# One tile's receptance projected from two scaled inputs, a clamp taken into Relu and maximum, and scan columns filled by GpSimd: a layer of RWKV time mixing and a gated feed-forward block on one Trainium2 core

## The reference

```python
x = x + attn(layernorm(x));  x = x + ffn(layernorm(x))

# attn: x_prev is x shifted by one token, zero at the start
xk = x*tmk + x_prev*(1-tmk);  xv = x*tmv + x_prev*(1-tmv);  xr = x*tmr + x_prev*(1-tmr)
k, v, r = xk @ Wk.T, xv @ Wv.T, sigmoid(xr @ Wr.T)
# recurrence over tokens, per channel, p starts at -inf, q at 0
new_p     = max(p, u + k_t)
scale_old = exp(max(p - new_p, -30));  scale_cur = exp(max(u + k_t - new_p, -30))
wkv_t     = (scale_old*q + scale_cur*v_t) / (scale_old + scale_cur + 1e-9)
new_p2    = max(p + w, k_t)
q         = exp(max(p + w - new_p2, -30))*q + exp(max(k_t - new_p2, -30))*v_t
p         = new_p2
out       = (r * wkv) @ Wo.T

# ffn: ternary weights, hidden size 1024
h = silu(x@W1 * s1) * (x@W2 * s2);  h = gelu(h@H1 * sh1);  h = gelu(h@H2 * sh2);  out = h@W3 * s3
```

## Time and profile before

| what | value |
|---|---|
| time, median of 3 runs | 1485.84 us (1485.73 to 1486.19) |
| profiled execution | 1485.31 us |
| its span in the trace | 1483.6 us |
| TensorE busy | 1473.6 us, 99% of the span |
| VectorE busy | 1205.3 us, 81% |
| ScalarE busy | 1077.1 us, 73% |
| GpSimd busy | 204.3 us, 14% |
| memory read and written | 250.76 MB and 33.03 MB |

### The profile page before, as it was taken

How to read it: one execution, slowest core, us unless ns; L and a number is a source line. 1 busy time by engine, 2 the same in 40 slices (tenths; PEclk the granted TensorE clock), 3 DMA queues, 4 the chain that set the end, 5 groups by cost and what they waited for, 6 DMA issues and landing times.

```text
span 1483.6 us, 28137 instructions
## 1 busy us (share of the span) xinstructions
PE 1473.6 (99%) x10326; PEld 1324.7 (89%) x10326; DVE 1205.3 (81%) x1554; ACT 1077.1 (73%) x1626; POOL 204.3 (14%) x173
## 2 busy tenths in 40 slices
PE   8999999999999999999999999999999999999999
PEld 6989898998989989899898989989899898998998
DVE  7797887868888687887878878788886878878655
ACT  6895776867768777686867868677587776868655
POOL 1314020110201102011030210202011020110200
PEclk9999999999999999999999999999999999999999
DMA  9977474755737467374674746657475673746654
GB/s 352 380 264 270 148 231 118 222 160 171 242 97 242 125 204 227 106 248 117 203 210 130 235 130 205 176 168 227 103 240 139 193 234 97 250 117 201 192 178 140
DMA packets 94926, 285.28 MB, mean 192 GB/s; under 512 B 9136, under 2 KB 33328, under 8 KB 92976
## 3 DMA queue, kind: packets, MB, share of 16 engines
q1 hardware_dynamic: 86736, 277.01, 57.5%
q0 software_dynamic: 8160, 7.87, 4.5%
HBM read 250.76 MB, written 33.03 MB: 191 GB/s over the span
## 4 chain that ended last, share of the span: by engine, by line
PE 93%; DVE 3%; ACT 2%; issue 1%; POOL 1%; DMA 0%; DVEq 0%; POOLq 0%; ACTq 0%
PE acc L645 27%; PE acc L647 26%; PE att L554 10%; PE acc L619 7%; PE acc L620 7%; PE acc L671 4%; PE acc L673 4%; PE att L577 3%; PE att L533 2%; PE att L620 1%; PE att L619 1%; DVE stage L1724 1%; DVE op_lo L1595 0%; PE acc L773 0%; PE acc L771 0%
## 5 line engine op out<-in xcount | busy, mean ns | idle before, releaser
L645 PE MATMUL acc<-op_hi,ring 128*128 128x256 f32 x3360 | 810.7, 286 | 0.5 <-issue 0.5
L647 PE MATMUL acc<-op_lo,ring 128*128 128x256 f32 x3360 | 788.8, 279 | 0.0
L645 PEld LDWEIGHTS acc<-op_hi,ring 128*128 128x128 f32 x3360 | 632.2, 188 | 18.6 <-issue 17.6
L647 PEld LDWEIGHTS acc<-op_lo,ring 128*128 128x128 f32 x3360 | 632.0, 188 | 11.1 <-issue 10.0
L1595 DVE TENSOR_TENSOR op_lo<-blocks,op_hi 128x1024 fp32r<-128x1024 f32 (+2 forms) x271 | 338.9, 1265 | 98.3 <-ACT op_hi L1007 90.9
L1007 ACT ACTIVATE op_hi<-blocks 128x1024 fp32r<-128x1024 f32 (+2 forms) x263 | 283.7, 1091 | 82.8 <-DVE blocks L1590 74.9
L619 PE MATMUL acc<-x_hi,w_rnd 128*128 128x512 f32 x420 | 167.6, 399 | 0.0
L620 PE MATMUL acc<-x_lo,w_rnd 128*128 128x512 f32 x420 | 165.9, 395 | 0.0
L2018 POOL TENSOR_TENSOR v_sb<-mix_v,v_sb 128x1024 f32<-128x1024 f32 (+1 forms) x19 | 39.4, 2072 | 833.7 <-DVE r_sb L1522 824.8
L1047 ACT ACTIVATE blocks<-acc,vec 128x256 f32<-128x256 f32 x268 | 104.9, 475 | 60.9 <-PE acc L647 60.8
L1047 ACT ACTIVATE blocks<-parts,vec 128x256 f32<-128x256 f32 x240 | 102.3, 497 | 56.2 <-DVE parts L1652 47.9
(11 more groups left out here) (185 smaller groups left out, 2116.8 us busy)
## 6 DMA issues: line engine op xcount, KB each, us to landing
ring<-scratch SPq DMA_DIRECT2D x427, 512.0 KB, 4.2
scratch<-stage SPq DMA_DIRECT2D x11, 1024.0 KB, 12.4
stage<-in_w_ffn SPq DMA_DIRECT2D x10, 1024.0 KB, 10.9
x_in<-in_x SPq DMA_DIRECT2D x32, 256.0 KB, 4.8
out<-x_next SPq DMA_DIRECT2D x30, 256.0 KB, 5.1
out<-mix_v POOLq DMA_DIRECT2D x30, 256.0 KB, 4.4
scratch<-in_w_ffn SPq DMA_DIRECT2D x4, 1024.0 KB, 15.0
ring<-stage SPq DMA_DIRECT2D x7, 512.0 KB, 9.4
```

The costliest lines, as they stand in the source:

```text
L645: pe.matmul(out, act(w), act(op_hi[:, k, c, :]), start=(begins and c == 0 and m % 2 == 0), stop=False, skip_group_check=True)
L647: mm = pe.matmul(out, act(w), act(op_lo[:, k, c, :]), start=False, stop=(c == QC - 1), skip_group_check=True)
```

## The change

Only tile 0 is touched.

- Receptance of the first sequence. Instead of a `mix_r` made by VectorE, ScalarE makes two scaled copies of the transposed x straight from PSUM (`share_r`): x times tmr into `mix_r`, and x shifted by one column times (1 - tmr) into `share`, which lies in `x1_next`. TensorE projects both and adds them up in PSUM, eight matmuls where there were four. VectorE makes 1 - tmr (`rest_r`), and GpSimd sets the first column of `share` to zero. The late sequence's `ln1` moves ahead of the first key copies on ScalarE. A `sem_inc` on VectorE takes the place of the two missing counts of `dve_mix`.
- The clamp of the state's new share, in both sequences. It was a clamp to 0 and 30 on VectorE ahead of Exp(-x). Now ScalarE takes Relu of the exponent, then Exp(-x), and the bound of 30 comes as a maximum with exp(-30) in the multiplication by v. The other clamp on the same exponent comes after both exponents, and waits for Relu.
- The column 0 of `seq` is filled by GpSimd, in both sequences, once with the lowest number and once with zero, where VectorE copied `carry_p` and `carry_q`.

```diff
@@ -34,6 +34,7 @@
 WKV_EPS = 1e-9
 WARM = (17, 1, 9)
 CLAMP = 30.0
+LEAST_GAIN = float(np.exp(np.float32(-CLAMP)))
 LOWEST = float(np.finfo(np.float32).min)
 
 
@@ -207,6 +208,7 @@
         moments = sb("moments", [P, NB, 2])
         var_eps = sb("var_eps", [P, NB])
         minus_half = sb("minus_half", [P, NB])
+        rest_r = sb("rest_r", [P, DC])
         mean_neg = sb("mean_neg", [P, NB])
         rstd = sb("rstd", [P, NB])
         offset = sb("offset", [P, NB])
@@ -278,6 +280,7 @@
             return ap.rearrange("p (b d) -> p b d", b=NB)
 
         now, before = seq[:, :, :, 1:], seq[:, :, :, 0:SEG]
+        share = x1_next[:, 0:DC, 0:SEG]
 
         def ffn_weights(w):
             a = 0
@@ -352,6 +355,8 @@
         st_x1 = tally("st_x1", n_seq, 16)
         dve_last, st_last, pe_block = (ctx.enter_context(nc.semaphore(n)) for n in ("dve_last", "st_last", "pe_block"))
         first_scan = ctx.enter_context(nc.semaphore("first_scan"))
+        first_rest, first_share, first_relu = (ctx.enter_context(nc.semaphore(n)) for n in ("first_rest", "first_share", "first_relu"))
+        first_col = ctx.enter_context(nc.semaphore("first_col"))
         first_wo = ctx.enter_context(nc.semaphore("first_wo"))
         first_x1 = ctx.enter_context(nc.semaphore("first_x1"))
         first_num = ctx.enter_context(nc.semaphore("first_num"))
@@ -545,14 +550,23 @@
                 for j in chunks:
                     which, e = divmod(j, DC)
                     src = (mix_k, mix_v, mix_r)[which]
-                    pe.wait_ge(s.dve_mix.sem, s.dve_mix.at(t, (which + 1) * DC))
+                    if s is FIRST[0] and which == 2:
+                        pe.wait_ge(first_share, 1 + 2 * DC)
+                    else:
+                        pe.wait_ge(s.dve_mix.sem, s.dve_mix.at(t, (which + 1) * DC))
+                    if s is FIRST[0] and which == 1:
+                        pe.wait_ge(first_share, 1 + 2 * DC)
                     if s is WHOLE and j >= 2:
                         pe.wait_ge(s.act_kvr.sem, s.act_kvr.at(t, j - 1))
                     elif j >= 4:
                         pe.wait_ge(s.act_kvr.sem, s.act_kvr.at(t, j - 3))
                     for c in range(DC):
                         mm = pe.matmul(s.banks[KVR_BANK[j]][:, s.cols], wm[:, which, c, e * P:(e + 1) * P], src[:, c, s.cols],
-                                       start=(c == 0), stop=(c == DC - 1))
+                                       start=(c == 0), stop=(c == DC - 1 and not (s is FIRST[0] and which == 2)))
+                    if s is FIRST[0] and which == 2:
+                        for c in range(DC):
+                            mm = pe.matmul(s.banks[KVR_BANK[j]][:, s.cols], wm[:, which, c, e * P:(e + 1) * P], share[:, c, :],
+                                           start=False, stop=(c == DC - 1))
                     s.pe_kvr.add(mm)
 
             def project_out(s, t):
@@ -946,6 +960,14 @@
                 act.wait_ge(s.act_x.sem, s.act_x.at(t, 3))
                 s.act_x.add(act.activation(carry_x[:, :, s.seqs], seq[:, :, s.seqs, SEG:SEG + 1], ACT.Copy))
 
+            def share_r(s):
+
+                act.wait_ge(first_rest, 1)
+                for c in range(DC):
+                    x = s.banks[c][:, s.cols]
+                    act.activation(mix_r[:, c, s.cols], x, ACT.Identity, scale=tmr[:, c:c + 1]).then_inc(first_share, 1)
+                    act.activation(share[:, c, 1:SEG], x[:, 0:SEG - 1], ACT.Identity, scale=rest_r[:, c:c + 1]).then_inc(first_share, 1)
+
             def copy_kvr(s, t, chunks=range(3 * DC)):
                 for j in chunks:
                     which, e = divmod(j, DC)
@@ -958,6 +980,9 @@
 
                 act.wait_ge(s.dve_pre.sem, s.dve_pre.at(t, (1, 2, 3, 4)[k] if isinstance(t, int) and t < 2 else (3, 4, 1, 2)[k]))
                 ap, sign = ((fresh, -1.0), (norm_ch, 1.0), (mix_v, 1.0), (mix_k, -1.0))[k]
+                if s is not WHOLE and k == 0:
+                    act.activation(fresh[:, :, s.cols], norm_ch[:, :, s.cols], ACT.Relu).then_inc(first_relu, 1)
+                    act.wait_ge(first_relu, 1 + FIRST.index(s))
                 s.act_exp.add(act.activation(ap[:, :, s.cols], ap[:, :, s.cols], ACT.Exp, scale=sign))
 
             def exp_r(s, t):
@@ -1164,8 +1189,9 @@
             act.activation(warm_act[:], zeros[:], ACT.Exp)
             ln1(early_seq, 0)
             copy_x(early_seq, 0)
+            share_r(early_seq)
+            ln1(late_seq, 0)
             copy_kvr(early_seq, 0, [0, 1])
-            ln1(late_seq, 0)
             exp(early_seq, 0, 0)
             exp(early_seq, 0, 1)
             copy_kvr(early_seq, 0, range(2, 3 * DC))
@@ -1427,10 +1453,11 @@
 
             def first_running_max(s):
 
+                if s is FIRST[0]:
+                    dve.wait_ge(s.dve_mix.sem, s.dve_mix.at(0, 2 * DC))
+                    dve.sem_inc(s.dve_mix.sem, DC)
                 dve.wait_ge(s.dve_mix.sem, s.dve_mix.at(0))
                 dve.wait_ge(s.act_x.sem, s.act_x.at(0))
-                link(s, dve.tensor_copy(seq[:, :, s.seqs, 0:1], carry_p[:, :, s.seqs]))
-                settle(s, 0)
                 n = s.pairs[0]
                 for c in range(DC):
                     dve.wait_ge(s.pe_kvr.sem, s.pe_kvr.at(0, c + 1))
@@ -1452,8 +1479,11 @@
                 k4, p4 = by_seq(k_sb[:])[:, :, s.seqs], before[:, :, s.seqs]
                 for c in range(DC):
                     if s is not WHOLE:
+                        if c == 0:
+                            dve.wait_ge(first_col, 1 + 2 * FIRST.index(s))
                         dve.wait_ge(s.act_kvr.sem, s.act_kvr.at(t, c + 1))
-                    link(s, dve.scalar_tensor_tensor(by_seq(norm_ch)[:, c, s.seqs], p4[:, c], decay[:, c:c + 1], k4[:, c], ALU.add, ALU.subtract))
+                    done = link if s is WHOLE or c < DC - 1 else lambda s, instruction: s.dve_pre.add(instruction)
+                    done(s, dve.scalar_tensor_tensor(by_seq(norm_ch)[:, c, s.seqs], p4[:, c], decay[:, c:c + 1], k4[:, c], ALU.add, ALU.subtract))
 
             def exponents(s, t):
                 now_exponents(s, t)
@@ -1482,10 +1512,12 @@
             def first_exponents(s, t):
 
                 next_exponents(s, t)
-                settle(s, t)
-                next_clamps(s, t, 0)
                 now_exponents(s, t)
                 settle(s, t)
+                g = norm_ch[:, :, s.cols]
+                dve.wait_ge(s.dve_pre.sem, s.dve_pre.at(t, 1))
+                dve.wait_ge(first_relu, 1 + FIRST.index(s))
+                s.dve_pre.add(dve.tensor_scalar(g, g, 0.0, -CLAMP, ALU.min, ALU.max))
                 now_clamps(s, t, 2)
 
             def gain(s, t):
@@ -1494,13 +1526,19 @@
                 if s is FIRST[0]:
                     dve.wait_ge(s.act_kvr.sem, s.act_kvr.at(t, 2 * DC))
                 new = fresh[:, :, s.cols]
+                if s is not WHOLE:
+                    link(s, dve.scalar_tensor_tensor(new, new, LEAST_GAIN, v_sb[:, :, s.cols], ALU.max, ALU.mult))
+                    return
                 link(s, dve.tensor_tensor(new, new, v_sb[:, :, s.cols], ALU.mult))
 
             def recurrence(s, t, c):
 
                 if c == 0:
                     settle(s, t)
-                    link(s, dve.tensor_copy(seq[:, :, s.seqs, 0:1], carry_q[:, :, s.seqs]))
+                    if s is WHOLE:
+                        link(s, dve.tensor_copy(seq[:, :, s.seqs, 0:1], carry_q[:, :, s.seqs]))
+                    else:
+                        dve.wait_ge(first_col, 2 + 2 * FIRST.index(s))
                 for n in s.pairs:
                     link(s, dve.tensor_tensor_scan(
                         now[:, c, n, :], by_seq(norm_ch)[:, c, n, :], by_seq(fresh[:])[:, c, n, :],
@@ -1771,9 +1809,10 @@
             first_variance(late_seq)
             dve.wait_ge(ld_vec, 16)
             dve.wait_ge(setup_pool, 2)
+            dve.tensor_scalar(rest_r[:], tmr, -1.0, 1.0, ALU.mult, ALU.add).then_inc(first_rest, 1)
             mix_difference(early_seq, 0)
-            for which in range(3):
-                mix(early_seq, 0, which)
+            mix(early_seq, 0, 0)
+            mix(early_seq, 0, 1)
             first_running_max(early_seq)
             first_exponents(early_seq, 0)
             gain(early_seq, 0)
@@ -2057,11 +2096,18 @@
             pool.memset(zeros[:], 0.0)
             pool.memset(carry_x[:], 0.0)
             pool.memset(carry_q[:], 0.0)
+            pool.memset(share[:, :, 0:1], 0.0).then_inc(first_share, 1)
             pool.memset(carry_p[:], LOWEST).then_inc(setup_pool, 1)
             pool.wait_ge(setup_pool, 2)
             for k, s in enumerate(FIRST):
                 first_deviation(s, 1 + k)
             for k, s in enumerate(FIRST):
+                column = seq[:, :, s.seqs, 0:1]
+                pool.wait_ge(s.dve_mix.sem, s.dve_mix.at(0))
+                pool.memset(column, LOWEST).then_inc(first_col, 1)
+                pool.wait_ge(s.dve_pre.sem, s.dve_pre.at(0, 3))
```

(2 more changed lines are left out.)

## The result

The changed kernel takes 1488.3 us (median of 20 runs, 1486.24 to 1490.41), the kernel before beside it 1485.8 us (20 runs, 1484.71 to 1488.52). The ratio is 1.0014, with a 95% interval of 1.0008 to 1.0021. By the medians it is 2.5 us more and by the means 2.1, which lies within the 0.2% (3.0 us) that the prediction took as the bound of "no change". The forecast, 1486.5 us, had the direction right. Its range ended at 1487.6 and does not hold the time.

What follows compares the result with a forecast made beforehand. TensorE, busy 99% of the span, was taken as the bound. Tile 0's delay of +0.66 us grows to +0.87, less 0.2 at the transposes: +0.7, so a median of 1486.5 us, range 1485.2 to 1487.6.

Steps and rivals of the forecast that it cites:

- The first sequence: Tile 0's front: VectorE gains 0.4 to 0.5 us, but the doubled receptance projection makes x1 0.66 us late.
- a loss of this part alone: Relu on ScalarE replacing VectorE's clamp in tile 0: 0.63 us against the clamp's 0.43.
- The second sequence: Tile 0 behind the x1 copy: 0.66 us late grows to +0.87, less 0.2 at the transposes, giving +0.7 us.
- the forecast of +0.87: Second sequence: Exp of the remaining clamp starts 0.87 us late, and the second check frees TensorE as late.
- it will not move: Weight transfer landing at 56.78 us, before the second sequence's transposes: its queue waits for no arithmetic, so it stays put.
- the second wait for a check: TensorE after the transposes: a wait for a load its own matmuls release, so the delay would fill none of it.
- the 0.3 us for op_lo: TensorE's later wait for op_lo, 0.3 us: follows its own earlier work, so the delay would not fill it.
- the prediction's own signs of being wrong: x1 copied before 27.1, TensorE past the transposes before 60.1, or a granted clock below 1.00.
- (1): Tile 0's front keeps its time, gain and loss cancel: 1485.8 us, 1485.4 at best; chance 0.22.
- (2): SyncE's load of tile 1's x, issued at 48.08, moves with transfers behind it: 1487.3 us; chance 0.13.
- (3): TensorE's clock halves at the wait before 51.13 until the transposes, adding 5.9 us: 1492.4 us; chance 0.02.
- (4): Relu brings table loads of 1.28 us each; the instruction order shows none added; chance nil.

Runs made afterwards that it cites:

- e16: The kernel before with feed-forward loads held until the last ring piece lands, plus the change's Relu and GpSimd columns, without the doubled receptance: 1486.19 us.
- e7: The kernel before with half of the second set's receptance projection moved ahead of TensorE's third flag check: 1487.72 us, against 1486.30 for the kernel before.
- the held pair: The kernel before and the changed kernel, both with SyncE's feed-forward loads held until the last ring piece has landed: means 1485.98 and 1486.90 us.
- e3: The kernel before with ten warming matmuls instead of nine ahead of the first output projection: 1486.93 us, ratio 1.0010.
- e2: The kernel before with only the first sequence's receptance from two scaled copies and eight matmuls: 1487.43 us, ratio 1.0011.
- e19: The changed kernel again, unaltered, against the kernel before: 1488.17 us, ratio 1.0005.
- e1: The changed kernel with the first sequence's receptance made as before, Relu and GpSimd's columns kept: 1486.76 us, ratio 1.0005.
- e6: The changed kernel with SyncE holding the feed-forward loads back until the last ring piece has landed: 1486.42 us.

## Why the prediction was right and wrong

**The first sequence, right.** Forecast and measured: exponents of the scan ready for the clamps at 14.55, and Relu started at 14.48; Relu 0.63 for 128x512, exactly as taken from Exp; scaled copies 0.46 to 0.48 each at a pitch of 0.36, against 0.4 taken; second receptance copy done at 18.33 forecast and 18.26 measured; warming from 18.4, measured 18.32; x1 at 27.7, measured 27.64. ScalarE's idle time held the four copies, as said. The scan started at 11.94 after 0.53 us of waiting for the key chunk, also as said. The sentence from the Trainium skill ("ScalarE: Activation LUTs"), that relu belongs on VectorE, was put down as a loss of this part alone. e16 bears it out: +0.47 us at x1.

**The second sequence, right but for one term.** Exp of the remaining clamp: 35.87 forecast, 35.63 measured; table load 38.5 and 38.26. The second check freed TensorE at 52.19, where the forecast of +0.87 gave 52.00, though everything before had been 0.25 early. One low part of an operand on VectorE took longer, in a stretch where GpSimd works too, as it does in the kernel before; why it took longer is not shown. Before, and in the changed kernel:

```profile
41.08 0.69 DVE L1595 TENSOR_TENSOR op_lo<-blocks,op_hi 128x512 fp32r<-128x512 f32 x1
```

```profile
41.74 1.16 DVE L1633 TENSOR_TENSOR op_lo<-blocks,op_hi 128x512 fp32r<-128x512 f32 x1
```

The transposes came at 60.24 (60.3 forecast) and took 0.60 us, as forecast, not 0.84. The w_rnd transfer did not stand still, as I had claimed with "it will not move": its check began at 56.78 before and at 55.42 after, at 57.49 in e7. It decided nothing here.

**What failed** is one sentence of the part on the second sequence: "From there TensorE has no stop that this would fill: the second wait for a check (a load that its own matmuls release) and the 0.3 us for op_lo follow its own earlier work". The wait is released by its own matmuls, that is true, and it was 0.23 us. But I took its length for a constant. It is the lag of a transfer that shares the engines with 4 MB of others, and that lag is anything from 4.0 to 6.8 us. In the changed kernel's profile it added 1.36 us, and the clock after it 1.45 (some 0.8 net). A granted clock below 1.00 stood among the prediction's own signs of being wrong. The wait for op_lo, which I also left out of play, is the one that the delay filled:

```profile
137.86 0.39 PE L671 MATMUL acc<-w_rnd,op_hi 128*128 128x256 f32 x1 [0.29 <-DVE op_lo L1595]
```

**The sum.** Forecast +0.7 us; at 60 us the profile had +0.57 to +0.82, and the held pair, where the rest is taken out, +0.9 by the runs. So the term that I had was sized right, within the 0.5 to 1.3 that the runs allow. The term that I did not have is about 0.65 us by the means of all runs (0.05 to 1.3), and 1.36 and 1.45 us at its places in the profiled execution. Beside that, the spread of the runs was put at 0.3 us, from three runs; 156 runs show 22% of the kernel before's executions more than 1.4 us above its median. The kernel before's median itself moved by 1.1 us between groups. This too made the range narrow.

**The rivals.** (1), that gain and loss cancel: the 1.72 us of doubled matmuls decided against it, as stated. (2), that the delay grows through transfers behind SyncE's load of tile 1's x: right in kind, since transfers did the growing, wrong in place and size. The load that it names went out at 48.14, where it had gone out at 48.08. (3), that TensorE's clock falls: it did fall, but at the third check, and for 1.45 us, not 5.9, since it came back within some 4 us. At the second check TensorE waited 0.94 us and the clock stayed. (4), table loads: none was added. **Chances.** "Within 0.2%" had 0.96 and held. The range left no room for a combination of (2) and (3).

**What stays open.** The counts (68% of the changed kernel's runs above 1487.5 us, against 22%, and 26% and 6% when held) fit a late landing that is more frequent with the change, but do not show it: the front's delay and its lost slack also move runs over that line, and runs without a profile have no lag to read. Nor is it shown why a delay of 0.6 us should make it so: SyncE issues the four transfers at the same distance behind the ring piece in both kernels. e3, with a delay and nothing else, has a higher mean too (1.55 us above the kernel before of its group), but its profile shows no late landing. Whether another split of the transfers would end it for good was not tried.

## What to carry to other kernels

A wait that looks short and is released by the engine's own work can still have a transfer in it. Read that transfer's time from issue to landing in more than one execution, and what else is in the queues then, before taking the wait as a constant. If a stall is filled on one engine, look for the in-order engine that feeds it: ScalarE's own wait for the same load was the second path, and removing the first alone gained nothing. A change that fills an engine's wait may also take the slack that had absorbed a late load. Where a change is worth less than the spread of single runs, compare fixed points of the profiles and pooled runs; three runs do not show a tail.

## What the runs showed of the hardware

**The clock does not follow from the length of one wait.** TensorE waited 1.58 us in the changed kernel's profile and its clock fell to half; it waited 2.75 us in e2's, in the same place, and it did not. At the front, where TensorE waits for its first mixing weights, e2 waited 2.09 us at full clock, and the second run of the changed kernel (e19) 2.01 us, after which the clock fell. These are e19's TensorE rows and windows:

```profile
10.54 1.13 PE L535 MATMUL acc<-wm,ident 128*128 128x512 f32 x2 [2.01 <-DMA wm<-in_w_mix]
11.50 3.57 PE L564 MATMUL acc<-mix_k,wm 128*128 128x256 f32 x8
```

```profile
10.00:12.00 2.00, 1.46 (x4) 0.89 (x5) 1.44 (x4) 1.68 (x4) 0.10 (x1) 0.89 1.03 422
12.00:14.00 2.00, 2.00 (x6) 1.57 (x5) 0.50 (x1) 0.00 (x0) 0.00 (x0) 0.50 0.99 418
14.00:16.00 2.00, 2.00 (x9) 1.68 (x8) 1.11 (x4) 0.43 (x2) 0.00 (x0) 0.76 1.03 434
```

The key projection takes 3.57 us there instead of 1.99, and that execution is 3 us late at 27 us already. How often this happens can't be told from the mean clock that each run lists. Of the kernel before's 136 runs in the four groups, 30 list one below 1.00, with a median of 1488.07 us against 1485.86 of the others, and 9 of the changed kernel's 31. But e2's profiled execution lists 0.999, and its granted clock is 1.00 in every window up to its last matmul: it falls at 1487 us, when only the last store is waited for.

**The first load varies.** TensorE's wait for the mixing weights was between 0.34 and 2.09 us in the 18 profiles.

**The last store has two lengths.** SyncE's wait for it at the end of the program (us in total, times, longest us) was, in the kernel before and in e1,

```profile
SPq L157 <- DMA out<-mix_v: 1.4, 1, 1.4
```

```profile
SPq L158 <- DMA out<-mix_v: 2.7, 1, 2.7
```

It was 1.4 or 1.5 us in most profiles, 2.7 or 2.8 in four (e1, e3, e6, e19), 3.2 in e2, and nothing between. So e1 and e3 end 1.3 us later than VectorE's last operation would have them, for a reason that no edit made. Part of the kernels' spread of single runs is this.
